# One batch's steps in a new order on four engines: gated cross-attention and a channel-mix FFN

## The reference

```python
# x (16, 512, 512); ctx (16, 120, 512); weights 512 x 512; 16 heads of 32; all float32
def attention(q_in, ctx):                       # per batch
    Q, K, V = q_in @ W_q.T, ctx @ W_k.T, ctx @ W_v.T     # split into 16 heads
    s = Q K^T / sqrt(32) - slope[h] * (query_pos - key_pos)
    s = where(mask == 0, -inf, s)
    e = exp(s - max(s))
    return (e / (1 + sum(e)) @ V) @ W_o.T
def ffn(x):
    xr = mu_r * x + (1 - mu_r) * shift(x)       # shift: the token before, zero for the first
    xk = mu_k * x + (1 - mu_k) * shift(x)
    return sigmoid(xr @ W_r) * (relu(xk @ W_k) ** 2 @ W_v)
x = x + tanh(g_xattn) * attention(layernorm(x), ctx)
x = x + tanh(g_ffn) * ffn(layernorm(x))
```

## Time and profile before

| | |
|---|---|
| median of 3 runs | 1474.18 us (1472.98 to 1476.51) |
| profiled execution | 1474.89 us, span 1473.1 us |
| PE busy | 1372.3 us, 93% |
| DVE busy | 1128.0 us, 77% |
| ACT busy | 891.0 us, 60% |
| POOL busy | 720.5 us, 49% |
| DMA | 45 GB/s mean |

### The profile page before, as it was taken

How to read it: one execution, slowest core, us unless ns; L and a number is a source line. 1 busy time by engine, 2 the same in 40 slices (tenths; PEclk the granted TensorE clock), 3 DMA queues, 4 the chain that set the end, 5 groups by cost and what they waited for, 6 DMA issues and landing times.

```text
span 1473.1 us, 34107 instructions
## 1 busy us (share of the span) xinstructions
PE 1372.3 (93%) x11584; PEld 1143.7 (78%) x11584; DVE 1128.0 (77%) x2745; ACT 891.0 (60%) x2928; POOL 720.5 (49%) x766
## 2 busy tenths in 40 slices
PE   7988999999999999999999999999999999999988
PEld 6876778778787877878787787878787787878767
DVE  5447868787887878788786879878687878878675
ACT  5247475665747476674747566574756657474752
POOL 0003555645555554555555465545556455555542
PEclk9999999999999999999999999999999999999999
DMA  8721002020100102011010201111010201101000
GB/s 270 220 80 38 26 17 64 0 53 26 49 29 28 50 0 79 0 49 29 28 50 14 64 0 49 29 40 39 28 51 0 64 15 49 29 28 42 3 29 29
DMA packets 53010, 65.97 MB, mean 45 GB/s; under 512 B 23024, under 2 KB 29168, under 8 KB 52976
## 3 DMA queue, kind: packets, MB, share of 16 engines
q1 hardware_dynamic: 52976, 65.52, 14.9%
HBM read 40.87 MB, written 24.64 MB: 44 GB/s over the span
## 4 chain that ended last, share of the span: by engine, by line
PE 36%; DVE 28%; issue 17%; POOL 9%; ACT 6%; DMA 2%; DVEq 1%; SPq 0%; POOLq 0%; ACTq 0%
PE rotating L417 26%; DVE diff L1144 4%; DVE probs_room L1082 4%; DVE mix_k L1136 4%; POOL probs_room L1362 4%; PE score_bank L417 3%; PE probs_bank L584 3%; ACT probs_room L824 3%; POOL norm L1400 2%; DVE relu L1144 2%; PE attn_bank L598 2%; DVE stats L1049 2%; DVE norm L1061 2%; DVE xs L1105 2%; POOL mixed_gate L1395 1%
## 5 line engine op out<-in xcount | busy, mean ns | idle before, releaser
L824 ACT ACTIVATE probs_room<-probs_room 128x121 f32<-128x121 f32 x1024 | 392.1, 388 | 28.5 <-DVE probs_room L1086 28.5
L1362 POOL TENSOR_TENSOR probs_room<-probs_room,recip 128x960 f32<-128x960 f32 x128 | 229.7, 1795 | 209.4 <-DVE recip L1094 209.4
L417 PE MATMUL rotating<-w_proj,attn_t 128*128 128x512 f32 x768 | 207.6, 409 | 21.0 <-ACT gated L875 19.0
L1082 DVE SCALAR_TENSOR_TENSOR probs_room<-mask_in,score_bank 128x120 f32<-128x120 f32 x1024 | 212.9, 270 | 3.3 <-issue 0.3
L417 PE MATMUL rotating<-mixed_key,w_key 128*128 128x256 f32 x1440 | 198.5, 289 | 11.0 <-ACT gated L875 11.0
L417 PE MATMUL rotating<-w_value,xnt_or_act 128*128 128x512 f32 x720 | 202.7, 410 | 6.4 <-DVE xs L1105 6.4
L831 ACT COPY probs_room<-probs_bank 120x512 f32<-120x512 f32 x256 | 150.0, 586 | 82.0 <-PE probs_bank L584 80.4
L417 PE MATMUL rotating<-xnt_or_act,w_query 128*128 128x256 f32 x1536 | 198.8, 286 | 0.5 <-DVE xnt_or_act L1067 0.5
L417 PEld LDWEIGHTS rotating<-mixed_key,w_key 128*128 128x128 f32 x1440 | 178.6, 191 | 22.0 <-ACT gated L875 17.3
L824 ACT ACTIVATION_READ_ACCUMULATOR probs_room<-probs_room 128x1 f32 x1024 | 195.0, 190 | 0.0
L417 PEld LDWEIGHTS rotating<-xnt_or_act,w_query 128*128 128x128 f32 x1536 | 187.8, 191 | 1.9 <-DVE xnt_or_act L1067 0.8
(11 more groups left out here) (121 smaller groups left out, 2109.7 us busy)
## 6 DMA issues: line engine op xcount, KB each, us to landing
xs<-in_x_dram SPq DMA_DIRECT2D x64, 256.0 KB, 2.9
out_dram<-gated SPq DMA_DIRECT2D x64, 256.0 KB, 3.0
value_scratch<-gated SPq DMA_DIRECT2D x16, 240.0 KB, 2.7
mask_in<-in_mask_dram SPq DMA_DIRECT2D x16, 240.0 KB, 3.3
keys_t<-key_scratch SPq DMA_DIRECT2D x16, 240.0 KB, 2.6
values<-value_scratch SPq DMA_DIRECT2D x16, 240.0 KB, 4.2
probs_room<-in_ctx_t_dram SPq DMA_DIRECT2D x6, 480.0 KB, 7.4
key_scratch<-query_t SPq DMA_DIRECT2D x12, 240.0 KB, 4.9
```

The source lines that it names most:

```text
L417: mm = pe.matmul(bank, stationary(a, c), moving(b, c), start=(i == 0), stop=(i == MATMULS - 1))
L824: e = act.activation(row, row, ACT.Exp, bias=neg_max[:, t % 2, head:head + 1], scale=-1.0, accum_out=sums[:, t % 2, head:head + 1])
L1082: z = dve.scalar_tensor_tensor(out=probs[:, t % 2, head, :], in0=far, scalar=-SLOPES[head], in1=score_banks[j][:, g * NK:(g + 1) * NK], op ...
L1362: pool.tensor_tensor(part, part, recip[:, t % 2, heads].unsqueeze(2).to_broadcast((P, H // 2, NK)), ALU.mult)\
```

## The change

On each of PE, ACT, DVE and POOL the list of steps in `batch` is written in another order. No step, buffer, semaphore or wait condition differs; on PE some uses are cut into other ranges, and some products are laced into each other. The lists before stand above. The diff, cut to its core (a line that stays is without a sign):

```diff
 # PE
+use("gate", 0, range(0, 1))
 scores(b, 0, g) for all g
-use("gate", 0); use("gate", 1); use("key", 0)
+use("gate", 0, range(1, 12)); use("gate", 1, range(0, 11))
+use("key", 0, range(0, 1)); use("gate", 1, range(11, 12)); use("key", 0, range(1, 12))
 scores(b, 1, g)
-use("key", 1)
+use("key", 1, range(0, 8))
 turn_probs(b, 0, 0)
+use("key", 1, range(8, 12))
 use("key", 2, range(0, 3)) ... turn_probs(b, 0, 3), use("key", 2, range(9, 12)), attend(b, 0, g)
-use("key", 3)
 scores(b, 2, g)
+use("key", 3)
 use("proj", 0)
-use("value", 0)
+use("value", 0, range(0, 8))
 turn_probs(b, 1, 0)
-use("value", 1, range(0, 3))
+use("value", 0, range(8, 12))
 turn_probs(b, 1, 1)
-use("value", 1, range(3, 6))
+use("value", 1, range(0, 5))
 turn_probs(b, 1, 2)
-use("value", 1, range(6, 9))
+use("value", 1, range(5, 9))
 turn_probs(b, 1, 3), use("value", 1, range(9, 12)), attend(b, 1, g), scores(b, 3, g)
 use("gate", 2), use("turn2", 0)
-use("proj", 1)
+use("proj", 1, range(0, 10))
 turn_probs(b, 2, 0)
-use("value", 2, range(0, 3))
+use("value", 2, range(0, 2)); use("proj", 1, range(10, 12)); use("value", 2, range(2, 3))
 turn_probs(b, 2, 1)
 use("value", 2, range(3, 6))
+use("gate", 3, range(0, 1))
 turn_probs(b, 2, 2), use("value", 2, range(6, 9)), turn_probs(b, 2, 3)
-use("value", 2, range(9, 12))
+use("value", 2, range(9, 12)) laced with use("gate", 3, range(1, 4))
 attend(b, 2, g)
-use("gate", 3); use("turn1", 0); use("turn2", 1)
-turn_probs(b, 3, 0) ... turn_probs(b, 3, 3), with use("proj", 2) in threes behind each
+turn_probs(b, 3, 0)
+use("gate", 3, range(4, 10)); use("turn2", 1); use("gate", 3, range(10, 12)); use("proj", 2, range(0, 2))
+turn_probs(b, 3, 1)
+use("proj", 2, range(2, 4)); use("turn1", 0); use("proj", 2, range(4, 6))
+turn_probs(b, 3, 2)
+use("proj", 2, range(6, 12))
+turn_probs(b, 3, 3)
 attend(b, 3, g), use("turn1", 1), use("value", 3)
-use("proj", 3); use("turn1", 2); use("query", 0); use("turn2", 2); use("query", 1, range(0, 7))
-use("turn1", 3); use("query", 1, range(7, 12)); use("turn2", 3)
+use("proj", 3) laced with use("query", 0, range(0, 2)); use("turn1", 2)
+use("query", 0, range(2, 8)); use("turn2", 2); use("query", 0, range(8, 12))
+use("query", 1, range(0, 7)); use("turn1", 3); use("query", 1, range(7, 9)); use("turn2", 3)
+use("query", 1, range(9, 12))
 use("query", 2), use("query", 3)
 # ACT
-feed_forward((gate_out, 1)) ahead of exps(b, 0, 1)
+feed_forward((gate_out, 1)) behind exps(b, 0, 1)
-act_split 0, relu_out 1, probs_out(b, 0, 0), (b, 0, 1), act_split 1, probs_out(b, 0, 2), (b, 0, 3), relu_out 2
+act_split 0, probs_out(b, 0, 0), (b, 0, 1), (b, 0, 2), relu_out 1, probs_out(b, 0, 3), act_split 1, relu_out 2
-attn_out(b, 0), exps(b, 1, 0), act_split 2, relu_out 3, exps(b, 1, 1) with act_split 3 in it, exps(b, 1, 2), (b, 1, 3)
+attn_out(b, 0), exps(b, 1, 0), (b, 1, 1), (b, 1, 2), relu_out 3, exps(b, 1, 3), act_split 2
-probs_out(b, 1, 0), (b, 1, 1), exps(b, 2, 0, front)
+exps(b, 2, 0, front), probs_out(b, 1, 0), (b, 1, 1)
-attn_out(b, 1) ahead of exps(b, 2, 1)
+attn_out(b, 1) behind exps(b, 2, 2); act_split 3 behind gate_out 2
-gate_out 3, probs_out(b, 3, 0), turn1_out 0, probs_out(b, 3, 1), turn2_out 1, probs_out(b, 3, 2),
-mix_key_high 0, probs_out(b, 3, 3), mix_gate_high 0, attn_out(b, 3), turn1_out 1
+probs_out(b, 3, 0), gate_out 3, probs_out(b, 3, 1), turn1_out 0, probs_out(b, 3, 2),
+mix_key_high 0, turn2_out 1, probs_out(b, 3, 3), turn1_out 1, attn_out(b, 3), mix_gate_high 0
-mix_key_high 2, mix_gate_high 2, query_out 3
+mix_key_high 2, query_out 3, mix_gate_high 2
 # DVE, behind attn_low(b, 0)
-distances(b + 1), reciprocals(b, 1, 0), bias(b, 2, 0), residual 0, reciprocals(b, 1, 1), bias(b, 2, 1 to 3),
-statistics2 0, finish 0, normalise2 0, attn_low 1, reciprocals(b, 2, 0), finish 1, statistics1 0,
-reciprocals(b, 2, 1), bias(b, 3, 0), bias(b, 3, 1), normalise1 0, bias(b, 3, 2), residual 1, statistics2 1,
-reciprocals(b, 3, 0), bias(b, 3, 3), finish 2, normalise2 1, attn_low 2, statistics1 1, reciprocals(b, 3, 1),
-mix_key 0, mix_gate 0, turn1_low 0, normalise1 1, statistics1 2, residual 2, attn_low 3, turn1_low 1,
-normalise1 2, statistics2 2, finish 3, normalise2 2, residual 3, turn1_low 2, statistics1 3, statistics2 3,
-normalise1 3, normalise2 3, turn1_low 3, mix_key 1, mix_gate 1, mix_key 2, mix_gate 2, mix_key 3, mix_gate 3
+bias(b, 2, 0), bias(b, 2, 1), reciprocals(b, 1, 0), bias(b, 2, 2), residual 0, statistics2 0, reciprocals(b, 1, 1),
+finish 0, distances(b + 1), bias(b, 2, 3), normalise2 0, finish 1, reciprocals(b, 2, 0), bias(b, 3, 0), attn_low 1,
+statistics1 0, reciprocals(b, 2, 1), bias(b, 3, 1), bias(b, 3, 2), residual 1, bias(b, 3, 3), reciprocals(b, 3, 0),
+statistics2 1, statistics1 1, normalise1 0, normalise2 1, finish 2, attn_low 2, reciprocals(b, 3, 1), mix_key 0,
+turn1_low 0, normalise1 1, residual 2, mix_gate 0, statistics1 2, turn1_low 1, attn_low 3, statistics2 2, finish 3,
+normalise1 2, normalise2 2, residual 3, mix_key 1, turn1_low 2, statistics1 3, statistics2 3, normalise1 3,
+normalise2 3, turn1_low 3, mix_gate 1, mix_key 2, mix_gate 2, mix_key 3, mix_gate 3
 # POOL, behind squared_relu 2
-squared_relu 3, act_rest 2, act_rest 3, normalise_probs(b, 1, 0), (b, 1, 1), rstd2_of 0, normalise_probs(b, 2, 0),
-rstd1_of 0, normalise_probs(b, 2, 1), edge 0, difference 0, rstd2_of 1, normalise_probs(b, 3, 0), (b, 3, 1),
-rstd1_of 1, edge 1, difference 1, rstd1_of 2, mix_key_low 0, mix_gate_low 0, rstd2_of 2
+normalise_probs(b, 1, 0), squared_relu 3, normalise_probs(b, 1, 1), rstd2_of 0, normalise_probs(b, 2, 0),
+act_rest 2, act_rest 3, normalise_probs(b, 2, 1), edge 0, difference 0, rstd1_of 0, normalise_probs(b, 3, 0),
+rstd2_of 1, normalise_probs(b, 3, 1), rstd1_of 1, rstd1_of 2, mix_key_low 0, edge 1, rstd2_of 2, difference 1,
+mix_gate_low 0
 rstd1_of 3, rstd2_of 3, edge 2, difference 2, mix_key_low 1, mix_gate_low 1, edge 3, difference 3
-mix_key_low 2, mix_gate_low 2
+mix_gate_low 2, mix_key_low 2
 mix_key_low 3, mix_gate_low 3
```

More of the change, by code:

```diff
@@ L670, in batch @@
                 use("turn2", 0)
-                use("proj", 1)
+                use("proj", 1, range(0, 10))
                 turn_probs(b, 2, 0)
-                use("value", 2, range(0, 3))
+                use("value", 2, range(0, 2))
+                use("proj", 1, range(10, 12))
+                use("value", 2, range(2, 3))
                 turn_probs(b, 2, 1)
                 use("value", 2, range(3, 6))
+                use("gate", 3, range(0, 1))
                 turn_probs(b, 2, 2)
@@ L678, in batch @@
                 turn_probs(b, 2, 3)
-                use("value", 2, range(9, 12))
+                use("gate", 3, range(1, 2))
+                use("value", 2, range(9, 11))
+                use("gate", 3, range(2, 3))
+                use("value", 2, range(11, 12))
+                use("gate", 3, range(3, 4))
                 for g in range(G):
                     attend(b, 2, g)
-                use("gate", 3)
-                use("turn1", 0)
[L684 to L688, removed]
+                turn_probs(b, 3, 0)
+                use("gate", 3, range(4, 10))
+                use("turn2", 1)
+                use("gate", 3, range(10, 12))
+                use("proj", 2, range(0, 2))
+                turn_probs(b, 3, 1)
+                use("proj", 2, range(2, 4))
+                use("turn1", 0)
+                use("proj", 2, range(4, 6))
                 turn_probs(b, 3, 2)
-                use("proj", 2, range(6, 9))
+                use("proj", 2, range(6, 12))
                 turn_probs(b, 3, 3)
-                use("proj", 2, range(9, 12))
                 for g in range(G):
@@ L696, in batch @@
                 use("value", 3)
-                use("proj", 3)
+                use("proj", 3, range(0, 7))
+                use("query", 0, range(0, 1))
+                use("proj", 3, range(7, 12))
+                use("query", 0, range(1, 2))
                 use("turn1", 2)
-                use("query", 0)
+                use("query", 0, range(2, 8))
+                use("turn2", 2)
+                use("query", 0, range(8, 12))
                 if last:
@@ L702, in batch @@
                     gate(b, 0, range(MATMULS), tail_bank).then_inc(done["gate"], 1)
-                use("turn2", 2)
                 use("query", 1, range(0, 7))
                 use("turn1", 3)
-                use("query", 1, range(7, 12))
+                use("query", 1, range(7, 9))
                 use("turn2", 3)
+                use("query", 1, range(9, 12))
                 use("query", 2)
@@ L928, in batch @@
                 exps(b, 1, 0)
[L929 to L930 removed]
                 exps(b, 1, 1, front)
[L932 removed]
                 exps(b, 1, 1, back)
                 exps(b, 1, 2)
+                feed_forward((relu_out, 3))
                 exps(b, 1, 3)
+                feed_forward((act_split, 2))
+                exps(b, 2, 0, front)
                 probs_out(b, 1, 0)
                 probs_out(b, 1, 1)
```

(5 more changed lines are left out.)

86 lines of the change are left out of this document (44 added, 42 removed).

## The result

The changed kernel takes 1411.64 us (median of 4 runs, 1410.31 to 1413.91) against 1473.58 for the kernel before, run beside it: a ratio of 0.958 [0.956, 0.960]. 62 us are gone, where 77 were forecast. The profiled execution took 1411.27 us at a granted clock of 0.998, before and after alike.

What follows compares the result with a forecast made beforehand. PE bounds the kernel: 76 us own work, 2.95 waits and 0.5 handovers give a 79.4 us batch, 5.2 less. Fourteen batches (73) and batch 15 (4) make 77: 1474.18 to 1397 us, own range 1380 to 1416, with first rival 1378 to 1440.

Steps and rivals of the forecast that it cites:

- PE's own work: PE's time per loop batch without waits: taken as 76 us, between readings of 74.9 and 76.9.
- the rounds: PE: four transposes, ACT's copy, the next four, only three product steps between; each round of 1.33 us loses 0.26.
- Scores 1 and tile 0: PE's waits at the front of a batch: 0.1 us at scores 1, 0.9 and 0.2 in tile 0.
- bias(0,0) at 4.4: DVE at the front of a batch: bias(0,0) comes 4.4 us after gate 0's first step, mix_key(1) having left the chain.
- POOL's last three subtractions ... covered: POOL at the batch's end: they end 5.7 us into the next batch, its next task comes at 10, so no cost.
- the third rival: DVE mix steps, mix_gate(0) to bias(0,0): POOL holds them more often; eight more holds give 1520 us; chance 0.08.
- turn_probs 2 of tile 0 keeps 0.9: PE in tile 0 waits 0.9 us for POOL's normalise_probs(0,1), with squared_relu(0) and act_rest(0) still ahead of it.
- The turns: PE's new waits in tile 3: 0.45 us at turn1 3 and 0.1 at turn2 3, from mix_key(1)'s new place on DVE.
- The rule weighed: DVE and POOL lock each other out for whole instructions; a new order could draw new lots for every mix step.
- Only the ends move: Rival: the batch's front stays bound by DVE and POOL; 2.6 us a batch gained, 1436 us; chance 0.18.
- The waits change places: Rival: diff(1) comes late for mix_key(1), DVE stands, turn1 3 is delayed; 1472 to 1477 us; chance 0.04.
- Slower by holds: Rival: POOL holds DVE's mix steps from mix_gate(0) to bias(0,0) more often; 1520 us with eight more holds; chance 0.08.

Runs made afterwards that it cites:

- The run in threes: The changed kernel with tile 1's transposes laced as before, three steps of value 1 behind each: 1419.26 us, ratio 0.963.
- the fastest version: The changed kernel with three waits added on POOL, for normalise2(2), mix_key(1) and mix_gate(3), mix_key(1) where the change put it: 1368.30 us, ratio 0.930.

## Why the prediction was right, and where 15 us went

The sign and the mechanism held: no instruction changed, and the gain is in waits of PE that went.

**What was sized rightly.** PE's own work with its small waits: 76 and 0.95 (0.2 and 0.2 at tiles 0 and 2, 0.1 and 0.3 at attend 1 and 3, 0.15 at proj 3) and 0.5 of handovers are 77.45; the fastest version's 77.79, less its one wait of 0.34, is 77.45. That it fits to the last digit is luck: 76 was chosen between two readings, and the lower has a slip (144 steps at 0.23 are 33.1 and not 33.7, so 74.3 and not 74.9). How the 77.45 divides is not shown. The run in threes says that the rounds lost less than 0.26, and so that the own work is rather higher and the small waits lower. Proj 1 waits 0.34 (0.45 forecast). value 3's wait for residual is gone, and no wait for bias(2,3) or act_rest(3) came. In the tail, key 0's 3.3 gave way to waits of 1.60 and 0.57, together just over the 0 to 2 that key 2 was given. Batch 15 gained 6.2 where 4 stood, and what lies before batch 1 gained 2.9, where -3 to +3 was taken as 0.

**What failed: two terms of the loop batch.** The batch is 80.70, not the 79 to 80 that would have shown the forecast right. Taken from the runs:

- Scores 1 and tile 0 were 0.1, 0.9 and 0.2. They cost 1.87 (80.70 against 78.83 when POOL waits for mix_gate(3)); tile 0's hidden 0.2 may not be in this, so the miss is 0.7 to 0.9. The step that failed is "bias(0,0) at 4.4": it came at 5.36. In the kernel before it came 6.30 behind the start of the batch on PE; less the 1.13 of mix_key(1) that is 5.2, and how the prediction came to 4.4 it doesn't show. The holds make up 0.2: from mix_gate(1) to bias(0,0) DVE takes 11.47 (649.37 to 660.84) and took 11.28 (677.08 to 688.36). In it mix_gate(1) and (2) became 1.06 and 1.02 shorter, mix_key(2) and mix_gate(3) 1.06 and 1.22 longer. "POOL's last three subtractions ... covered" was true for POOL; that they run on beside mix_gate(3) only the third rival says, and no price in the forecast stands for it. What the whole hold on mix_gate(3) costs, the old part of it too, is the 1.87. "turn_probs 2 of tile 0 keeps 0.9" was right in size (1.00) and half right in cause: with bias(0,0) 3.2 earlier it keeps nothing.
- The turns were 0.45 and 0.1. They cost 1.06 (80.70 against 79.64 when POOL waits for the normalisations), 0.5 too little. The step is the chain "proj 3 ends at 65.3, residual(3) 66.4": two normalisations in front of residual(3), taken at 0.55 each, took 1.27 and 1.50. The trace of before has such a duration among its normalisations (highest 1.31), and the prediction did not use it.

Proj 1 gives back 0.1. Together 1.1 to 1.3, about the whole of the miss in a batch (80.70 less 79.4). The loop brought 54.5 of its 73, the ends 9.1 of their 4: 63.6 between the profiled executions, 62 between the medians.

**The rule weighed.** The prediction said "by the rows alone the chain keeps its present holds", and set the other outcome aside as a rival of slower. In sum that nearly held: the chain in front of bias(0,0) grew by 0.2, but its holds moved to other places. Over the whole span the mix instructions are 9 us shorter and the normalisations 11 longer; most of DVE's 19 us less is in the second instruction of finish (65.2 to 48.5). Four mix instructions that nothing holds take 1.13 to 1.14 and not 1.36, so that the holds of before on mix_gate(2) and (3) were 2.8 and 2.0, where the prediction has 2.5 and 1.7. "mix_gate steps longer than before" was one of its signs of being wrong, and for mix_gate(3) it came. The Trainium skill (SBUF — State Buffer, Who interferes with whom) has the exclusive lock between a DVE instruction with two SBUF inputs and a GpSimd one that reads SBUF; for the mix steps the runs agree (4.32 to 1.14 when POOL's operations come later). The same section of the Trainium skill lets a DVE instruction with at most one SBUF input contend only in a two-port mode. A normalisation, one tensor and two scalars per partition, was held here (1.27 and 1.50 against 0.55); whether it runs in such a mode no run shows.

**The rivals.** "Only the ends move" fell: the rounds behind the front no longer wait as they did (the weight loads, 5.9 to 2.3 a batch), and the rival had let only 0.8 of that go, in tile 1. But its reason, the front bound by DVE and POOL, was half right, and is where a part of the next 43 us lay. "The waits change places" fell as it was meant: mix_key(1) starts at 643.16 without idle time ahead, so DVE does not stand for diff(1). Waits did change places once, by the move of mix_key(1), which is worth nothing clear of the noise. "Slower by holds" had the right mechanism and looked at a part of the list: the mix steps from mix_gate(0) on did not lose in sum, only mix_key(2) and mix_gate(3) did, and the normalisations, which it does not name.

## What to carry to other kernels

When an order is written anew, check each pair of DVE and POOL instructions that comes to lie side by side, and price it at the duration that the trace shows for the pair, not at the median: here POOL beside mix_gate(3) and beside the two normalisations cost 2.9 us of each 80.7. An engine with slack can be told to wait: three waits on POOL, 52% busy, took 3% off a kernel bound by PE. Lists that hand over to each other must be changed together: PE's alone cost 35 us, where all four brought 62.

## What was not expected of the hardware

- Beside POOL's tensor operations of 1.3 to 1.5 us, a DVE normalisation of 0.55 took 1.27 and 1.50, and four mix instructions of 1.14 in all took 4.32; POOL's own subtraction, 1.30 to 1.35 beside mix_gate(3), took 1.29 with DVE's mix out of the way (its difference(1) went further, from 1.41 beside the normalisation to 1.04 behind it):

```profile
1197.68 1.29 POOL L1412 TENSOR_TENSOR mixed_gate<-diff,mixed_gate 128x512 fp32r<-128x512 f32 x1 [2.72 <-DVE relu L1161]
```

- In the run with DVE's list of before, the granted clock fell to 1.2 GHz where PE met a wait of 3.1 us, after shorter ones close ahead of it: busy for 4.16 of 8 us, PE was then at 0.50 for 4.28 us in nine of the loop's 14 batches, and at 0.61 to 0.69 in the other five. The run with PE's new list alone takes 87.03 a batch, with its waits spread, and its clock is 0.998 over the span.
